# First-norm statistics in tile groups, second norm on ScalarE, four small factors on GpSimd, and a new order of work

## The reference, cut to what matters

```python
x = x + attn(layernorm(x), W_qkv, W_out)        # 16 heads of 16, causal
x = x + xattn(layernorm(x), ctx, mask)          # one head; softmax(x.ctx/16) @ ctx
x = x + ffn(layernorm(x), gate_w, down_w, g1, g2)
# ffn: rms_norm, rounding to integers by 127/max|x|, ternary weights,
#      h = gate*sigmoid(gate)*up, then the same for the down projection (704 -> 256)
```

## Time and profile before

| | us |
|---|---|
| median of 3 runs | 246.31 (243.99 to 248.69) |
| the profiled execution | 246.74 |
| its span, first to last instruction | 244.9 |
| busy PE, DVE, ACT, POOL | 199.6, 196.5, 140.5, 126.7 |
| mean granted TensorE clock | 0.944 |

### The profile page before, as it was taken

One profiled execution on the slowest core, in us unless ns is written; L12 is line 12 of the kernel. 1 busy time (PEld: TensorE's weight loads), 2 busy tenths in 40 slices (PEclk: granted clock), 3 DMA queues, 4 the chain that ended last, 5 costly groups with the idle time before them and its releaser, 6 DMA issues. The chain is left out here.

```text
span 244.9 us, 11759 instructions
## 1 busy us (share of the span) xinstructions
PE 199.6 (81%) x4512; PEld 153.4 (63%) x4512; DVE 196.5 (80%) x635; ACT 140.5 (57%) x390; POOL 126.7 (52%) x231
## 2 busy tenths in 40 slices
PE   4812797889688989898989898989898999856754
PEld 4712685768476767676767777777777776533432
DVE  2001364977699999999999999999999999999981
ACT  2104694445566667675758584848484757644541
POOL 8306401544264646464646465555556438586760
PEclk9985899999999999999999999999999999995695
DMA  6995000010110101111010101020102010000011
GB/s 184 357 343 173 3 3 5 5 46 5 44 28 23 40 31 31 41 24 41 23 43 21 46 12 54 0 65 1 64 0 66 0 64 27 26 0 4 21 50 57
DMA packets 11524, 12.68 MB, mean 52 GB/s; under 512 B 1057, under 2 KB 10849, under 8 KB 11489
## 3 DMA queue, kind: packets, MB, share of 16 engines
q1 hardware_dynamic: 11424, 12.24, 15.9%
q0 software_dynamic: 64, 0.00, 0.0%
HBM read 10.14 MB, written 2.10 MB: 50 GB/s over the span
## 5 line engine op out<-in xcount | busy, mean ns | idle before, releaser
L1507 POOL TENSOR_TENSOR zh<-hh,gd 128x352 f32<-128x352 f32 x32 | 30.2, 947 | 31.9 <-DVE hh L1097 31.9
L1472 POOL TENSOR_SCALAR ve<-mv 128x1 f32<-128x1 f32 x48 | 14.1, 294 | 42.2 <-issue 22.3
L306 PE MATMUL ps<-yaT,wqk 128*128 128x128 f32 x256 | 34.6, 292 | 0.5 <-ACT yaT L634 0.5
L306 PEld LDWEIGHTS ps<-yaT,wqk 128*128 128x128 f32 x256 | 32.1, 204 | 1.4 <-ACT yaT L634 0.9
L1474 POOL TENSOR_TENSOR rs<-ve,neghalf 128x1 f32<-128x1 f32 x48 | 29.3, 611 | 4.0
L290 PE MATMUL ps<-wg,zT 128*128 128x352 bf16 x128 | 26.3, 335 | 2.0 <-DVE x L1006 1.7
L930 DVE TENSOR_REDUCE mx<-ps 128x16 f32<-128x1024 f32 x16 | 19.5, 1220 | 9.9 <-PE ps L341 9.9
L657 ACT ACTIVATE kz<-ps,cst 128x256 f32<-128x256 f32 x32 | 14.8, 474 | 18.0 <-PE ps L306 18.0
L1529 POOL TENSOR_SCALAR hq<-zh,qh 128x704 f32<-128x704 f32 x16 | 13.6, 853 | 18.0 <-DVE qh L1133 17.9
L726 ACT ACTIVATE th_sb<-ps,th 128x352 f32<-128x352 f32 x32 | 17.8, 557 | 8.7 <-PE ps L290 3.7
L684 ACT ACTIVATE pT<-ps 128x512 f32<-128x512 f32 x32 | 17.4, 596 | 6.5 <-PE ps L377 6.5
(11 more groups left out here) (124 smaller groups left out, 536.4 us busy)
## 6 DMA issues: line engine op xcount, KB each, us to landing
ct_in<-ctx_t SPq DMA_DIRECT2D x16, 128.0 KB, 2.2
cn_in<-ctx_n SPq DMA_DIRECT2D x16, 128.0 KB, 2.2
out<-o_out SPq DMA_DIRECT2D x16, 128.0 KB, 1.7
wg<-gate_t SPq DMA_DIRECT2D x1, 1408.0 KB, 8.8
x_in<-x SPq DMA_DIRECT2D x1, 1280.0 KB, 10.3
wd<-down_t SPq DMA_DIRECT2D x1, 640.0 KB, 8.9
wqk<-wqkv_t SPq DMA_DIRECT2D x1, 512.0 KB, 3.9
x_in<-x SPq DMA_DIRECT2D x1, 512.0 KB, 8.6
```

What stands on the lines that cost most here:

```text
L306: last = pe.matmul(qk_ps[:, e * P:(e + 1) * P], wqk[:, c, e * P:(e + 1) * P], yaT[:, t % 2, c, :], start=(c == 0), stop=(c == DC - 1))
L1507: G.tensor_tensor(zh[:, t % 2, part], hh[:, t % 2, part], gd[:, part], ALU.mult).then_inc(ev[f"zh_d{j}"], 1)
```

## The change

1. **First norm in groups.** `stats_x(k)` and `rstd_x(k)` now handle groups of tiles (0), (1), (2, 3), (4 to 7), (8 to 15), which are also the DMAs of x. The statistics keep a slot for every tile. All groups are done by the third tile of attention on VectorE; GpSimd makes each factor for a whole group in one instruction, and `-mean` becomes an instruction of its own (`nm1`).
2. **Second norm on ScalarE.** `normalise_x1` leaves VectorE and becomes an activation with scale and bias; GpSimd makes its bias in a new `shift_x1`.
3. **Small factors.** `th`, `ea`, `ek` and `fd` move to GpSimd. `zm`, `qz`, `hm`, `qh` and `rvx` stay on VectorE but become `tensor_scalar`, and the constant tile `floor` goes.
4. **Loads.** x tile 1 is issued before `bits` and `wv`, x tiles 2 and 3 before the gate weights, `wout` and context 0 before the down weights. From context 5 on, a context load is issued one store earlier.
5. **PSUM banks and all orders.** Most PSUM tiles change bank, and all lists are written anew (of a list, the diff below shows the new order without the old lines); the loop now covers s = 6 to 13. On GpSimd, `set_v2` comes before the first `rstd_x`, `set_rest` after the first two. On ScalarE both weight sums stand together after the first exponentials.

```diff
+        st1, mv1 = sb("st1", [P, T, 6]), sb("mv1", [P, T, 2])
+        ve1, rs1, nm1, sh1 = [sb(n, [P, T]) for n in ("ve1", "rs1", "nm1", "sh1")]
...
-        xT_ps = ps[:, 2, 0:D]
-        qk_ps = ps[:, 2, 0:2 * D]
-        v_ps = ps[:, 1, 0:D]
-        mT_ps = ps[:, 5, 0:P // 2].bitcast(BF16)
-        o_ps = ps[:, 1, 0:PAIRS * 2 * VW].rearrange("p (i j d) -> p i j d", i=PAIRS, j=2)
-        oT_ps = ps[:, 7, 0:D]
-        y_ps = ps[:, 0, 0:D]
-        yxT_ps = ps[:, 2, 0:D]
-        sx_ps = ps[:, 1, 0:P]
-        pxT_ps = ps[:, 3, 0:P]
+        xT_ps = ps[:, 1, 0:D]
+        qk_ps = ps[:, 1, 0:2 * D]
+        v_ps = ps[:, 0, 0:D]
+        mT_ps = ps[:, 7, 0:P // 2].bitcast(BF16)
+        o_ps = ps[:, 2, 0:PAIRS * 2 * VW].rearrange("p (i j d) -> p i j d", i=PAIRS, j=2)
+        oT_ps = ps[:, 3, 0:D]
+        y_ps = ps[:, 3, 0:D]
+        yxT_ps = ps[:, 3, 0:D]
+        sx_ps = ps[:, 2, 0:P]
+        pxT_ps = ps[:, 6, 0:P]
         r_ps = ps[:, 3, 0:D]
         zT_ps = ps[:, 0, 0:D // 2].bitcast(BF16)
-        g_ps = [ps[:, 0, 0:HALF], ps[:, 4, 0:HALF]]
-        u_ps = [ps[:, 3, 0:HALF], ps[:, 6, 0:HALF]]
-        hT_ps = [ps[:, 2, 0:2 * P].bitcast(BF16), ps[:, 5, 0:(IC - 4) * P // 2].bitcast(BF16)]
-        d_ps = ps[:, 1, 0:D]
-        wtot_ps = ps[:, 5, 0:2]
+        g_ps = [ps[:, 1, 0:HALF], ps[:, 5, 0:HALF]]
+        u_ps = [ps[:, 0, 0:HALF], ps[:, 4, 0:HALF]]
+        hT_ps = [ps[:, 7, 0:2 * P].bitcast(BF16), ps[:, 2, 0:(IC - 4) * P // 2].bitcast(BF16)]
+        d_ps = ps[:, 6, 0:D]
+        wtot_ps = ps[:, 2, 0:2]
...
+        groups = [(0, 1), (1, 2), (2, 4), (4, 8), (8, T)]
+        x_ld, st1_d, var1, ve1_d, nm1_d, rstd1, sh1_d = [[sem(f"{n}_{k}") for k in range(len(groups))] for n in (
+            "x_ld", "st1_d", "var1", "ve1_d", "nm1_d", "rstd1", "sh1_d")]
...
             sp.dma_start(wqk[:, :, :], w3[:, :, 0:2 * D]).then_inc(wqk_in, 16)
+            load_x(1)
             sp.dma_start(c8[:, :], bits).then_inc(c8_in, 16)
             sp.dma_start(wv[:, :, :], w3[:, :, 2 * D:3 * D]).then_inc(wv_in, 16)
-            load_x(1)
+            load_x(2)
             sp.dma_start(wg32[:, :].rearrange("p (c n) -> p c n", c=DC),
                          gate_t.rearrange("(c p) n -> p c n", p=P)).then_inc(wg_in, 16)
+            sp.dma_start(wo[:, :, :], wout_t.rearrange("(c p) e -> p c e", p=P)).then_inc(wo_in, 16)
+            load_ctx(0)
             full = INTER // P
...
             def step(s):
+                transpose_ya(s + 1, ("h1_d0", s - 3))
+                project_v(s, ("hh_d0", s - 3))
+                transpose_max(s, ("hT_d0", s - 4))
+                cross_readout(s - 2, ("x1_d", s))
+                scores_k(s, ("hh_d1", s - 3), ("h1_d1", s - 3), ("pxT_d", s - 1), ("mT_d", s + 1))
                 project_qk(s + 1, ("yaT_d", s + 2))
+                transpose_z(s - 3, ("v_d", s + 1))
+                down(s - 5, ("exp_d1", s + 1))
+                transpose_yx(s - 1, ("x2_d", s - 1))
+                readout(s, ("hT_d1", s - 4))
+                scores_q(s + 1, ("exp_d0", s + 1), ("out_d", s - 4), ("exp_d1", s + 1))
+                gate_up_0(s - 3, ("q_d", s + 2), ("k0_d", s + 2), ("k1_d", s + 2), ("zT_d", s - 2))
+                transpose_readout(s, ("yxT_d", s))
+                cross_scores(s - 1, ("oN_d", s + 1))
+                gate_up_1(s - 3, ("mx_d", s + 2))
+                transpose_h_0(s - 4, ("mx_d", s + 2))
+                project_out(s, ("oT_d", s + 1))
+                transpose_cross_weights(s - 1, ("mx_d", s + 2))
+                transpose_h_1(s - 4, ("expx_d", s))
...
+            def normalise_x1(t):
+                act.wait_ge(ev["sh2_d"], t + 1)
+                act.wait_ge(ev["x1_d"], t + 1)
+                after(act, ev["yxT_ps"], t - 1)
+                nc.scalar.activation(yx[:, t % 2, :], x1[:, t, :], ACT.Identity, bias=col(sh2, t), scale=col(rs2, t)).then_inc(ev["yx_d"], 1)
...
             normalise_x(0)
             keep_yaT(0)
             normalise_x(1)
+            keep_k_0(0)
+            keep_k_1(0)
             keep_q(0)
+            keep_v(0)
+            normalise_x(2)
             keep_yaT(1)
             keep_max(0)
             keep_k_1(1)
             keep_q(1)
+            keep_k_0(1)
+            exponentials_0(0)
+            keep_yaT(2)
             exponentials_1(0)
             sum_gate()
+            sum_down()
+            keep_oT(0)
+            keep_k_0(2)
+            keep_q(2)
+            keep_max(1)
             keep_k_1(2)
             normalise_x(3)
             keep_v(1)
             exponentials_1(1)
             exponentials_0(1)
...
+            def stats_x(k):
+
+                tiles = range(*groups[k])
+                dve.wait_ge(x_ld[k], 16)
+                for t in tiles:
+                    V.bn_stats(st1[:, t, :], x_in[:, t, :]).then_inc(st1_d[k], 1)
+                for n, t in enumerate(tiles):
+                    dve.wait_ge(st1_d[k], n + 1)
+                    V.bn_aggr(mv1[:, t, :], st1[:, t, :]).then_inc(var1[k], 1)
...
-                V.scalar_tensor_tensor(out=col(zm, t), in0=col(am, t), scalar=col(rs3, t), in1=floor[:, :],
-                                       op0=ALU.mult, op1=ALU.max).then_inc(ev["zm_d"], 1)
+                V.tensor_scalar(col(zm, t), col(am, t), col(rs3, t), 1e-5, ALU.mult, ALU.max).then_inc(ev["zm_d"], 1)
...
+            for s in range(6, 14):
                 max_lo(s)
                 gated_1(s - 4)
+                residual_1(s - 1)
+                cross_guard(s - 2)
                 inner_1(s - 4)
+                residual_2(s - 2)
                 stats_x1(s - 1)
+                variance_x1(s - 1)
+                inner_largest(s - 4)
+                stats_x2(s - 2)
+                variance_x2(s - 2)
+                integers_z(s - 3)
+                ffn_input(s - 2)
+                scale_hm(s - 4)
+                scale_rhm(s - 4)
+                ffn_largest(s - 2)
                 residual_3(s - 5)
+                weight_sums_inverse(s)
+                scale_qh(s - 4)
+                normalise_readout(s)
+                maxima(s + 1)
+                integers_h(s - 4)
+                max_hi(s + 1)
+                cross_maxima(s - 1)
+                gated_0(s - 3)
+                scale_zm(s - 2)
+                scale_rz(s - 2)
+                max_rest(s + 1)
+                cross_sums_inverse(s - 1)
+                scale_qz(s - 2)
+                max_mid(s + 1)
+                inner_0(s - 3)
...
+            def rstd_x(k):
+
+                part, n = slice(*groups[k]), groups[k][1] - groups[k][0]
+                pool.wait_ge(var1[k], n)
+                G.tensor_scalar(ve1[:, part], mv1[:, part, 1], 1.0, EPS, ALU.mult, ALU.add).then_inc(ve1_d[k], 1)
+                G.tensor_scalar(nm1[:, part], mv1[:, part, 0], -1.0, None, ALU.mult).then_inc(nm1_d[k], 1)
+                pool.wait_ge(ve1_d[k], 1)
+                G.tensor_tensor(rs1[:, part], ve1[:, part], neghalf[:, 0:1].broadcast_to([P, n]), ALU.pow).then_inc(rstd1[k], 1)
+                pool.wait_ge(nm1_d[k], 1)
+                pool.wait_ge(rstd1[k], 1)
+                G.tensor_tensor(sh1[:, part], nm1[:, part], rs1[:, part], ALU.mult).then_inc(sh1_d[k], 1)
...
+            def shift_x1(t):
+                pool.wait_ge(ev["rstd2"], t + 1)
+                after(pool, ev["yx_d"], t - 1)
+                G.tensor_scalar(col(sh2, t), mv2[:, t % 2, 0:1], col(rs2, t), -1.0, ALU.mult, ALU.mult).then_inc(ev["sh2_d"], 1)
+            def scale_th(t):
+                pool.wait_ge(ev["zm_d"], t + 1)
+                if t == 0:
+                    pool.wait_ge(wmean_set, 1)
+                after(pool, ev["tanh_d0"], t - 1)
+                after(pool, ev["tanh_d1"], t - 1)
+                G.tensor_scalar(col(th, t), col(zm, t), 0.5 / 127, wmean[:, 0:1], ALU.mult, ALU.mult).then_inc(ev["th_d"], 1)
+            def scale_ea(t):
+                pool.wait_ge(ev["rz_d"], t + 1)
+                if t == 0:
+                    pool.wait_ge(wsc, 2)
+                after(pool, ev["ek_d"], t - 1)
+                G.tensor_scalar(col(ea, t), col(rz, t), wth2[:, :], col(rz, t), ALU.mult, ALU.mult).then_inc(ev["ea_d"], 1)
+            def scale_ek(t):
+                pool.wait_ge(ev["ea_d"], t + 1)
+                after(pool, ev["m2_d"], t - 1)
+                G.tensor_scalar(col(ek, t), col(ea, t), EPS / 4, col(ea, t), ALU.mult, ALU.mult).then_inc(ev["ek_d"], 1)
+            def scale_fd(t):
+                pool.wait_ge(ev["hm_d"], t + 1)
+                if t == 0:
+                    pool.wait_ge(wmean_set, 1)
+                after(pool, ev["out_d"], t - 1)
+                G.tensor_scalar(col(fd, t), col(hm, t), 1.0 / 127, wmean[:, 1:2], ALU.mult, ALU.mult).then_inc(ev["fd_d"], 1)
 
...
+            set_v2()
+            rstd_x_0()
+            rstd_x_1()
+            set_bits()
             set_rest()
-            rstd_x(0)
-            shift_x(0)
-            set_v2()
-            rstd_x(1)
```

(113 more changed lines are left out.)

871 lines of the change are left out of this document (433 added, 438 removed).

## The result

The changed kernel takes **235.78 us** (median of 4 runs, 235.14 to 237.5); the kernel before took 245.15 beside it. The ratio is 0.9643, 95% interval 0.9586 to 0.97: faster by 3.6%. The forecast was 231.9, range 224 to 241. The profiled execution took 235.14, its span is 233.3: 11.6 us less than before, of the 14.8 forecast.

A forecast was written before the change was run, and what follows sets the result against it. It took VectorE to be full in the steady steps (119.4 of 124.0 us busy), TensorE close behind, and the start held by one wait. 246.74 - 8.6 + 2.0 - 6.0 - 2.2 = 231.9 us; range 224 to 241.

The forecast's parts named there:

- The start: Up to the first maxima: the second tile no longer waits for the third one's data; -8.6 us, -7.5 to -9.7.
- Tiles 0 to 5: From maxima of tile 0 to tile 5: sum_down loses its cover, 1.7 us; +2.0 us, bounds 0 and +5.7.
- The ten steps: Steady loop, tiles 5 to 15: step falls from 12.40 to 11.8 us; -6.0 us in all, bounds -15 and 0.
- The ring: Steady step: TensorE's project_v to scores_q and VectorE's maxima to inner_0 wait on each other; 11.9 us a step.
- TensorE's floor: Steady step: TensorE's own work, without its 0.8 us of waits, needs about 11.6 us a step.
- GpSimd as victim: Steady steps: the four factors moved to GpSimd become victims of VectorE's wf, hb and zb; no size given.
- Rival A: Steady steps: TensorE sets no floor and the step falls to VectorE's 10.9 us; total 222.9 us; chance 0.10.
- Rival B: Start won, loop not: some result arrives later by what VectorE saves; total 237.9 us; chance 0.19.
- C: Start: its gap is filled again by weight sums, statistics and late code; total 240.5 us; chance 0.10.
- D: Steady steps: GpSimd stalls hb, max_hi, max_rest, max_mid between maxima and inner_0, ring 13.7 us; total 250.9 us; chance 0.08.
- The end: After maxima of tile 15: work taken off VectorE shortens it; -2.2 us, bounds 0 and -4.

The follow-up runs named there:

- the mended one: Kernel before, with only shift_x(1) and set_bits put ahead of rstd_x(2) in GpSimd's list: 238.98 us, ratio 0.9834.
- the two others near it: Changed kernel with normalise_x1 back on VectorE, 232.33 us; changed kernel with stats_x1, variance_x1 before residual_2 and ea, ek on VectorE, 232.37 us.

## Why the prediction was right, and where its sum was not

- **The start** (-8.6, measured -10.2): the mechanism was right, seen also in the kernel before with one operation moved, but it was not the whole: the other 3.6 us are VectorE's wait for the same load ahead of `maxima(0)`, and some by chance; I had it in the earlier trace rows and called the moved loads free, not needed. `project_qk(0)` took 2.70 us where I carried 3.75 over from the earlier trace rows, and `maxima(0)` followed the transpose by 1.36 us, not 2.23. In single executions of kernels with the changed start the first `maxima` lay from 13.80 to 16.48, so more than 1 us of this is chance; the old start gave 25.16 and, in the kernel with `fd` moved, 23.82.
- **Tiles 0 to 5** (+2.0, measured +0.95): inside its bounds; not taken apart. The changed kernel once more took 53.06 us here against 52.18, so the term is no surer than about 1 us.
- **The ten steps** (-6.0, measured -1.0): this is the mis-sized term. The steady step was right, 11.79 for 11.8. Against that pace the other four lose 0.46 (first), 2.25 (the stall, with the 0.53 in `scores_k`), 1.46 (the low clock) and 0.95 (last): 5.1 us, the whole miss. In the last step TensorE waits 0.4 us and is busy 12.28 of 12.74 (11.28 of 11.66 before): likely work taken ahead from the end. I multiplied one step by ten. The loop of before had no such stall, but its trace did have the same thing ahead of the loop, four times from 38 to 65 us and up to 2.05 us long:

```profile
62.27 0.57 PE L390 MATMUL ps<-v,pT 128*32 128x34 f32 x40
64.89 0.40 PE L390 MATMUL ps<-v,pT 128*32 128x34 f32 x24 [2.05 <-issue]
```

A rewrite of TensorE's list could move such a gap into the ten steps; the sum had no term for it.
- **The ring**: the number was right and the ring was wrong. I had it through `inner_0` and `project_v`; it goes through `residual_3`, GpSimd's five and `residual_2`. TensorE's floor was not 11.6 but 11.31, where five variants end. I had taken the floor as the step less its named waits; the busy time of the earlier trace rows, 11.44 a step, was the nearer number.
- **GpSimd as victim**: it happened, but not to the factors that I named. In the changed kernel `ea`, `ek`, `fd` and `th` have medians within 7 ns of their shortest. The victim is `m`, which had been on GpSimd before: 0.73 us beside `wf`, 0.37 to 0.38 in the steady steps of the kernels where it no longer meets `wf`, and it stands in the ring. The rule of the Trainium skill, "SBUF — State Buffer", section "Who interferes with whom", that a VectorE instruction with two SBUF inputs contends with a GpSimd instruction that reads SBUF, agrees with that. It also says that the first one blocks the other: `fd` in the kernel before fits, it ends at 120.02 us, as `zh` does (120.00); for `m` it can't be read, since by the record `m` starts 0.16 us before `wf`. On the other side `wf` fell from a median of 1031 to 486 ns, as the prediction had it.
- **Rival A** (VectorE's 10.9) is out: TensorE is full at 11.31. Weight-load busy, the measure that the Trainium skill prefers ("Perfetto Trace Analysis", section "Identifying the Most-Contended Engine"), was 94.2 of 123.0 us, 77%, and in the five full steps 46.17 of 56.59, 82%; no shorter step was reached in any run, so here matmul busy time was the one that bounded. **Rival B** (237.9: start won, loop not) comes nearer to the ten steps' -1.0 than the forecast's -6.0 does, but not by its mechanism: the pace was won. That the total still fell near the forecast is in part luck: the start gave 1.6 us more and tiles 0 to 5 cost 1 us less than forecast, against the 5 us missed in the loop. **C** and **D** are out: the gap did not fill again, and `max_mid` (`mh`) has a median of 168 ns in the ring that D feared for.
- **The end** (-2.2, measured -1.35): the size is not shown. It is the difference to one execution of the kernel before, 44.49 us; the mended one, with the same list there, took 43.38, hardly more than the changed kernel's 43.14. In the new order the relief is real, 3.7 us, but the new order gives most of it away at the end, which the sum had at nothing.

What the change is made of, then: start 10.2, of which one moved operation gives over half; everything but the moves (order, grouped statistics and what goes with them) 12.45 to 11.31 a step; moving the second norm and the factors gives up to 0.45 of that back and earns 3.7 at the end of the new order. Beside each other, all moves and none come to the same (236.0 and 236.11). Faster than both is the changed kernel with `residual_3` earlier, 232.06; the two others near it (232.33, 232.37) cannot be told from it.

## What to carry to other kernels

When the full engine is relieved, find the ring that closes next by following the new wait back through every engine, and look for an instruction in it that needs nothing of the one before it. Where two ways end within 0.1 us of each other, test them together: each alone shows nothing. Price a loop by its list of steps, not by one step times their number, and price a move separately in the loop and at the end, since the engine that it relieves may be full in only one of them.
